# Four of sixteen state indices of a selective scan get their input from a GpSimd multiply in the channels' own layout

## The reference, cut to what matters

```python
delta = jax.nn.softplus(dt + b_dt[None, :, None])
A = -jnp.exp(A_log)

def step(state, inp):
    d_t, b_t, c_t, u_t = inp
    dA = jnp.exp(d_t[..., None] * A)
    state = dA * state + (d_t * u_t)[..., None] * b_t[:, None, :]
    y_t = jnp.einsum('bdn,bn->bd', state, c_t)
    return (state, y_t)
```

## Time and profile before

| | |
|---|---|
| median of 3 runs | 1421.58 us (1421.44 to 1421.61) |
| the profiled execution | 1421.13 us |
| its span, first to last instruction | 1419.3 us |
| scan stage, first to last scan | 608.5 to 1401.7 us |
| one middle chunk | 100.7 us |
| PE, DVE, ACT, POOL busy in the whole span | 95%, 71%, 62%, 60% |

### The profile page before, as it was taken

One profiled execution on the slowest core, in us unless ns is written; L12 is line 12 of the kernel. 1 busy time (PEld: TensorE's weight loads), 2 busy tenths in 40 slices (PEclk: granted clock), 3 DMA queues, 4 the chain that ended last, 5 costly groups with the idle time before them and its releaser, 6 DMA issues.

```text
span 1419.3 us, 24153 instructions
## 1 busy us (share of the span) xinstructions
PE 1353.3 (95%) x8924; PEld 1080.8 (76%) x8924; DVE 1010.3 (71%) x1358; ACT 879.9 (62%) x1459; POOL 844.6 (60%) x474
## 2 busy tenths in 40 slices
PE   7999999999999999999899999999999999999998
PEld 4445559999999988957677777777778678678787
DVE  7755543232233343488998998998989989989897
ACT  3211121111111132589998999999999999999983
POOL 3222211222222212368978988888889889889994
PEclk9999999999999999999999999999999999999999
DMA  9921126676667664331531642623534524613522
GB/s 298 397 100 59 52 78 227 252 268 249 248 257 267 254 229 171 146 88 46 104 77 46 133 93 51 145 61 77 119 75 90 105 62 91 134 47 88 136 74 62
DMA packets 111012, 197.07 MB, mean 139 GB/s; under 512 B 57519, under 2 KB 84271, under 8 KB 106038
## 3 DMA queue, kind: packets, MB, share of 16 engines
q1 hardware_dynamic: 93814, 146.75, 31.2%
q0 software_dynamic: 17088, 48.85, 16.0%
HBM read 141.78 MB, written 31.00 MB: 122 GB/s over the span
## 4 chain that ended last, share of the span: by engine, by line
PE 70%; ACT 12%; DVE 12%; issue 5%; DMA 0%; DVEq 0%; SPq 0%; ACTq 0%
PE bank L1666 17%; PE bank L1840 9%; PE bank L1611 9%; PE bank L1679 9%; DVE hst L1509 6%; ACT dA L947 5%; PE bank L1860 5%; ACT dbuT L936 4%; PE bank L1720 4%; PE bank L1767 2%; PE bank L1848 2%; PE bank L1731 2%; PE bank L1750 2%; PE bank L1712 2%; PE bank L1641 2%
## 5 line engine op out<-in xcount | busy, mean ns | idle before, releaser
L1509 DVE TENSOR_TENSOR_SCAN hst<-dA,carry,bank 128x512 f32<-128x512 f32 x512 | 631.8, 1267 | 56.3 <-PE bank L1840 38.0
L740 POOL TENSOR_TENSOR hst<-hst,c_bc 128x2048 f32<-128x2048 f32 x127 | 543.0, 4308 | 57.9 <-DVE hst L1509 48.9
L947 ACT ACTIVATE dA<-delta,negA 128x512 f32<-128x512 f32 x512 | 353.5, 712 | 8.0 <-DVE hst L1509 7.5
L1840 PEld LDWEIGHTS bank<-ident,dbuT 128*128 128x128 f32 x2048 | 240.0, 141 | 139.3 <-issue 66.0
L1840 PE MATMUL bank<-ident,dbuT 128*128 128x128 f32 x2048 | 311.3, 276 | 32.7 <-DVE hst L1509 28.5
L936 ACT ACTIVATE dbuT<-duT,bT 128x512 f32<-128x512 f32 x382 | 268.9, 710 | 5.4 <-PE bank L1840 5.4
L1666 PEld LDWEIGHTS bank<-f_sb,w_gu 128*128 128x128 f32 x2240 | 256.0, 192 | 4.7 <-issue 2.1
L1666 PE MATMUL bank<-f_sb,w_gu 128*128 128x128 f32 x2240 | 256.9, 275 | 0.7 <-ACT f_sb L804 0.7
L1860 PE MATMUL bank<-ident,hst 128*128 128x128 f32 x1648 | 226.2, 273 | 0.0
L1860 PEld LDWEIGHTS bank<-ident,hst 128*128 128x128 f32 x1648 | 188.9, 141 | 0.0
L670 POOL TENSOR_TENSOR x_sb<-x_sb,neg_half 128x1 f32<-128x1 f32 x35 | 22.6, 647 | 271.4 <-DVE x_sb L1290 271.4
(11 more groups left out here) (220 smaller groups left out, 1656.0 us busy)
## 6 DMA issues: line engine op xcount, KB each, us to landing
w_gu<-in_w_gu SPq DMA_DIRECT2D x35, 2048.0 KB
c_bc<-c_rows SPq DMA_DIRECT2D x64, 512.0 KB, 4.1
hst<-hst POOLq DMA_DIRECT2D x23, 1026.0 KB, 8.6
sorted_x<-sg_a SPq DMA_DIRECT2D x12, 387.0 KB, 12.1
x_sb<-sorted_x SPq DMA_DIRECT2D x35, 129.0 KB
x_sb<-in_x SPq DMA_DIRECT2D x8, 512.0 KB, 7.7
w_d<-in_w_d SPq DMA_DIRECT2D x1, 4096.0 KB, 20.7
x_mix<-x_sb SPq DMA_DIRECT2D x1, 4096.0 KB, 30.5
```

Of the source, the lines that this page charges most:

```text
L740: pool.tensor_tensor(h[:, :, :CH], h[:, :, 1:], c, ALU.mult).then_inc(hc_ready, 1)
L947: act.activation(dA[:, at % DA_BUFS, :], delta[q % B][:, d, :], ACT.Exp, scale=negA[:, d, n:n + 1]).then_inc(dA_ready, 1)
L1509: v.tensor_tensor_scan(h[:, d, 1:], dA[:, at % DA_BUFS, :], bank[4 + u % 2][:], carry1[q % B][:, n, d:d + 1], ALU.mult, ALU.add).then_inc( ...
L1840: ins = pe.transpose(bank[4 + u % 2][:, i * P:(i + 1) * P], dbuT[(DS * q + n) % DBU_BUFS][:, i, d * P:(d + 1) * P], ident[:])
```

## The change

For the indices in `DIRECT` (0, 2, 6, 9; in the first chunk 3, 6, 9) du*B_n is made in the channels' own layout. SP copies B's row to all partitions (`b_bc`, one buffer; B's rows are now stored beside C's in `bc_all`), and POOL multiplies the whole du, kept in a tile of its own, by it in one instruction of 128x2048 (`make_dbu`), three states ahead. The scans of these indices read that buffer from SBUF and no bank. ACT spreads all twelve others, POOL none. The merges at 9 and 13 go; PE adds those states singly. `duT` and `bias_b` are kept once instead of twice, which makes room. The tables of units are new, and ACT's spreads and PE's turns have tables of their own (`ACT_SPREAD`, `PE_TURN`).

```diff
-POOL_SPREADS = (5, 6, 8, 11)
-SPREAD_LEAD = 4
+DIRECT = (0, 2, 6, 9)
+DIRECT_LEAD = 3
-MERGES = {1: 0, 9: 8, 13: 12}
-LAST_MERGES = {1: 0, 9: 8}
+MERGES = {1: 0}
+LAST_MERGES = {1: 0}
+FIRST_DIRECT = (3, 6, 9)
+LAST_DIRECT = (0, 2, 6, 9)
...
+        du = sb(l1, "du", [P, DB, CH])
+        b_bc = sb(l1, "b_bc", [P, CH])
...
+            def load_b(g):
+
+                if g in DIRECT_NO:
+                    q, n = divmod(g, DS)
+                    sp.wait_ge(c_stored, 16 * TPC * (q + 1))
+                    wait_past(sp, direct_made, DIRECT_NO[g])
+                    sp.dma_start(b_bc[:], bc_all[q:q + 1, n, :].broadcast_to([P, CH])).then_inc(b_loaded, 16)
...
                     wait_freed(pool, t, f"DL{d}")
-                pool.tensor_tensor(du[:, d, :], delta[(t + 1) % B][:, d, :], xc[:, d, :], ALU.mult).then_inc(du_ready, 1)
+                if t > 0:
+                    wait_full(pool, t - 1, f"DUT{d}")
+                if t >= 0:
+                    pool.wait_ge(direct_made, sum(g < DS * (t + 1) for g in DIRECT_NO))
+                to = du_first if t < 0 else du
+                pool.tensor_tensor(to[:, d, :], delta[(t + 1) % B][:, d, :], xc[:, d, :], ALU.mult).then_inc(du_ready, 1)
...
-            def spread_du(q, n):
...
+            def make_dbu(g):
+
+                wait_slot(pool, g)
+                if g >= DS:
+                    pool.wait_ge(du_ready, DB * (g // DS) + DB - 1)
+                pool.wait_ge(b_loaded, 16 * (DIRECT_NO[g] + 1))
+                rows = b_bc[:].unsqueeze(1).broadcast_to([P, DB, CH])
+                pool.tensor_tensor(dbuT[g % DBU_BUFS][:], du[:], rows, ALU.mult).then_inc(direct_made, 1)
...
+            pool.wait_ge(delta_first, DB)
+            pool.wait_ge(xc_ready, DB)
+            pool.wait_ge(down_ready, SLOTS)
+            pool.tensor_tensor(du[:], delta[0][:], xc[:], ALU.mult).then_inc(du_again, 1)
+            pool.wait_ge(du_again, 1)
...
                     if n in merges(q):
                         merge(q, n)
+                    if g + DIRECT_LEAD in DIRECT_NO:
+                        make_dbu(g + DIRECT_LEAD)
...
-                    v.wait_ge(dbu_full, at + 1)
+                    g = DS * q + n
+                    if g in DIRECT_NO:
+                        v.wait_ge(direct_made, DIRECT_NO[g] + 1)
+                        dbu = dbuT[g % DBU_BUFS][:, d, :]
+                    else:
+                        v.wait_ge(dbu_full, FULL[at])
+                        dbu = bank[4 + u % 2][:]
...
-                    v.tensor_tensor_scan(h[:, d, 1:], dA[:, at % DA_BUFS, :], bank[4 + u % 2][:],
+                    v.tensor_tensor_scan(h[:, d, 1:], dA[:, at % DA_BUFS, :], dbu,
                                          carry1[q % B][:, n, d:d + 1], ALU.mult, ALU.add).then_inc(scan_done, 1)
```

More of the change, by code:

```diff
@@ L150 @@
 CLAIMS = sorted(JOBS, key=lambda name: CLAIMED[name])
+ACT_ORDER, PE_ORDER = [[] for _ in range(UNITS * CHUNKS)], [[] for _ in range(UNITS * CHUNKS)]
+for q in range(CHUNKS):
+    units = [u for u in range(UNITS) if u // DB not in direct(q)]
+    planned = q > 0 and direct(q) == DIRECT
+    for k, u in enumerate(units):
+        at = u - AHEAD if not ACT_SILU + 1 < u - AHEAD <= ACT_SILU + PIECES else ACT_SILU + 1
+        if q or u >= 2 * TPC:
+            ACT_ORDER[UNITS * q + (ACT_SPREAD[k] if planned else at)].append((q, u))
+        if q or u > 2:
+            PE_ORDER[UNITS * q + (PE_TURN[k] if planned else u - 1)].append((q, u))
 FIRST_CLAIMS = {"X0": 5, "X1": 6, "X2": 5, "X3": 6, "XN0": 5, "XN1": 6, "DT": 5, "DL0": 5, "DL1": 6, "DL2": 5, "DL3": 6,
@@ L172, in tiles_of @@
     return slice(lo, lo + TPC)
-def pool_spreads(q):
-    return POOL_SPREADS if q + 1 < CHUNKS else LAST_SPREADS
+DIRECT_NO, SPREAD_NO, FULL = {}, {}, {}
+LAST_USER, bank_user = {}, [None, None]
+for g in range(DS * CHUNKS):
+    if g % DS in direct(g // DS):
+        DIRECT_NO[g] = len(DIRECT_NO)
+        continue
+    SPREAD_NO[g] = len(SPREAD_NO)
+    for d in range(DB):
+        at = DB * g + d
+        FULL[at] = DB * SPREAD_NO[g] + d + 1
+        LAST_USER[at], bank_user[at % 2] = bank_user[at % 2], at
 PLACE = {}
@@ L1021, in _ @@
                         decay(q, u + 1)
-                    if u == ACT_SILU + 1:
-                        for piece in range(u + AHEAD, u + AHEAD + PIECES):
-                            spread_du(q, piece)
-                    elif u + AHEAD < UNITS:
-                        if (q > 0 or u + AHEAD >= 2 * TPC) and not ACT_SILU + 1 < u <= ACT_SILU + PIECES:
-                            spread_du(q, u + AHEAD)
-                    elif q + 1 < CHUNKS:
-                        spread_du(q + 1, u + AHEAD - UNITS)
+                    for of, piece in ACT_ORDER[unit(q, u)]:
+                        spread_du(of, piece)
                     slot(q, u)
@@ L1829, in spread @@
                 n, d = divmod(u, DB)
-                on_pool = pool_spreads(q)
-                if d == 0 and n in on_pool:
-                    pe.wait_ge(dbuT_pool, TPC * (len(POOL_SPREADS) * q + on_pool.index(n) + 1))
-                elif d == 0:
-                    made = sum(k not in on_pool for k in range(n + 1))
-                    pe.wait_ge(dbuT_act, TPC * (DS - len(POOL_SPREADS)) * q + TPC * made - FIRST_PIECES)
-                    if q == 0 and n == 0:
+                g, at = DS * q + n, unit(q, u)
+                if g in DIRECT_NO:
+                    return
+                if d == 0:
+                    pe.wait_ge(dbuT_act, TPC * (SPREAD_NO[g] + 1) - FIRST_PIECES)
+                    if g == 0:
                         pe.wait_ge(dbuT_first, FIRST_PIECES)
-                wait_past(pe, scan_done, unit(q, u - 1))
+                if LAST_USER[at] is not None:
+                    pe.wait_ge(scan_done, LAST_USER[at] + 1)
                 for i in range(TPC):
```

156 lines of the change are left out of this document (78 added, 78 removed), and 11 rows, old and new, of the table SUM_AT.

## The result

The changed kernel takes 1613.05 us (median of 4 runs, 1612.7 to 1615.09), the kernel before 1421.51 us in the same runs: the ratio is 1.135, 95% interval 1.133 to 1.137. The forecast of 1585.8 us had the direction and the mechanism right and the size 27 us too low. The profiled execution took 1615.09 us, with a span of 1613.3, against 1421.13 and 1419.3 before: 194.0 us more.

What follows compares the result with a forecast made beforehand. PE, DVE and ACT were taken to set the period in turn. A middle chunk became 93.3 + 2 + 27.3 = 122.6 us; all chunks added 164.7 to 1421.1, giving 1585.8 us, range 1485 to 1645.

Steps and rivals of the forecast that it cites:

- one instruction a state: Rival: at each direct state DVE waits for one POOL instruction, +11.4 us a middle chunk, 1509 us; chance 0.13.
- every scan: Rival: exclusion at every direct scan, with POOL always holding another multiply, 1650 us; chance 0.09 near 1640.
- the three places: Earlier trace at 39.35, 36.66 and 584.86: DVE or POOL instructions held or lengthened beside the other, 584.86's from 0.40 to 3.56 us.
- The walk: POOL's list beside DVE's through a middle chunk's four direct states: 27.3 us of standing DVE.
- (a): State 6: DVE waits out 2.3 us of C(4), scans once, then waits 4.2 for C(5): 6.5 us lost.
- (b): State 9: DVE waits for 1.5 us of C(7), all of C(8) and a du piece of 1.3 us: 7.0.
- (c): State 0, POOL furthest behind: DVE waits for part of C(14), C(15) and index 2's multiply: 9.9 us.
- (d): State 2: DVE waits only for C(1), which starts some 0.3 us ahead of its arrival: 3.9 us.
- the credit for idle time: Middle chunk: PE and ACT catch up while DVE stands, so 2 of DVE's 7.4 us idle time remain.
- the sum: All chunks' growth added: five middle chunks +109.5, chunk 6 +22.5, first +12.8, last +19.9; +164.7 us in all.

Runs made afterwards that it cites:

- The second probe: The kernel before with six short DVE and POOL stages added behind its last store, some with a DMA issue ahead of POOL's multiplies; one scan stood 11.41 us.
- the 98.1 us chunk: The changed kernel with direct scans reading what is left in bank 4 or 5 instead of the SBUF buffer: 1410.08 us, ratio 0.992.
- the run that raised it: The changed kernel with PE also transposing du*B for the direct states, which nothing reads: 1627.64 us, ratio 1.145.
- the third kernel with the decay in a bank: The changed kernel with direct states' decays written to banks 4 and 5, two units later in ACT's list: 1487.48 us, ratio 1.047.

## Why the prediction was right, and where its sizes were off

**The mechanism.** It forecast that DVE and POOL exclude each other at the direct scans, with ends that coincide with POOL's, a direct mean of 2.5 us or more, bank scans at 1.27, C multiplies up to 1.2 us longer, and chunks of 112 to 128 us. Measured: 2.71, 1.27, 5.07 against 4.19, and 126. Two runs close the argument from both sides: the operand alone makes the kernel before slow (1542), and the changed kernel without it is fast (1410). The rivals with one instruction a state (1509) and with every scan (1650) fall with the 12.55 us scan and with the three free scans behind it. One of the three places that the forecast rested on was not of its kind: the instruction of 584.86 is a `tensor_scalar` with a single tensor in SBUF, and not a pair of two. The second probe shows that one held as well, so the reading did no harm.

**The holds.** The walk gave 27.3 us a middle chunk; DVE's busy time shows 23.0. By its letters, taken from each direct scan's length over 1.25: (a) state 6, 3.9 and not 6.5; (b) state 9, 4.6 and not 7.0; (c) state 0, 11.3 and not 9.9; (d) state 2, 3.5 and not 3.9. At 6 and 9 the walk had DVE arrive while an earlier C multiply had 2.3 and 1.5 us left. In the trace that one was over at 6, and at 9 the hold began with C(8). As I read it (no run took it apart), a hold keeps DVE back while POOL works off its backlog, and the walk carried the backlog of the old pace along. At 0, where most stands on POOL, it was the other way round. The first chunk lost 13.9 (walk: 17.4), the last 25.6 (25.5). Over the eight chunks DVE's busy time rose from 732.2 to 910.2 us, 178.0 us of standing, against 206.7 in the sum.

**The step that failed is the credit for idle time.** "PE and ACT catch up while DVE stands, so of the 7.4 us that DVE idles now I leave 2". DVE's idle time is 9.8 us in the middle chunk (126.1 less 116.3), 9.6, 9.3 and 9.3 in the first, seventh and last, nowhere less. Over the eight chunks it is 78.2 us, where it was 61.0 before and the sum left 19: 42 us of credit were given, and 17 were lost on top. Of these 59 us the smaller holds gave back 29, and what lies outside the chunks 1; the rest is the 29 us that the profiled execution lies above 1585.8. So the sum came as near as it did because two errors partly cancelled, which is luck. PE does not catch up in a hold. It stands too, 17.5 us a chunk in waits for scans, and starts when DVE starts; that it can't work ahead because its two banks are full and its additions wait for scans is read from the lists, and no run took it apart. A single hold a chunk already leaves DVE idle for 8.6 us and not 7.4. Without holds, in the 98.1 us chunk, the same lists have DVE idle for 5.6 us. Part of the wait may be the lower clock, whose transposes take 292 ns and not 275; the run that raised it also gave PE more to do, so that stays open.

**PE, ACT and POOL.** PE's busy time was to fall to 92.5 and 75% of a chunk; it rose to 100.0, 79%, at the clock of 0.89. At 1.00, in the kernel of 98.1 us, it is 92.9. ACT is at 95.2 (75%), as costed at nothing. POOL has 93.9 and not 91, mostly since its direct multiplies take 4.69 us and not 4.2. That is no wait for scans. In the third kernel with the decay in a bank, where no scan has both operands in SBUF, they take as long:

```profile
L763 POOL TENSOR_TENSOR dbuT<-du,b_bc 128x2048 f32<-128x2048 f32 x4 | 18.7, 4679 | 0.0
```

So the C multiply's 4.2 us was the wrong price for them. B's rows, the new waits and the single merge cost nothing that shows, as said.

## What to carry to other kernels

Before moving work to GpSimd, look at what VectorE reads meanwhile: in these runs a scan with one operand in PSUM did not notice GpSimd, and one with two in SBUF stood for the GpSimd instructions that read SBUF. The price is not a rate but GpSimd's backlog at that moment, so walk both lists in order and count what GpSimd still has queued, and give no credit for engines catching up unless their buffers let them run ahead. A buffer moved to PSUM to avoid this costs depth: two banks in place of eight buffers cost 77 us here at the best of three places and 152 at the worst, counted from the 1410 us kernel, of the port's 203.

## What was not expected of the hardware

- GpSimd lets a waiting VectorE instruction in between two of its own (its next multiply then takes 5.07 us instead of 4.16), but not always, and a DMA issue of its own ahead is neither needed for the exception nor enough. In the second probe one scan stood 11.41 us behind an issue, and in the changed kernel the first scan of all seven later chunks took 11.9 to 13.8 us, six of them behind an issue and the one of 11.94 without. With a quarter of the direct multiply, behind the same issue, a scan that arrived in GpSimd's second instruction was let in ahead of the third. The 3.56 us of the earlier trace rows may be another case: a DMA issue ends right ahead of POOL's three multiplies there. What decides is open.
- A `tensor_scalar` on VectorE with one SBUF tensor is held like a scan with two, in the second probe: 10.36 us behind an issue, where it takes 0.47 with GpSimd idle. Beside GpSimd's memset, which holds no scan, it took 0.97.
- GpSimd's short pieces take turns with VectorE: four pieces of 128x512 and three scans take 4.48 and 4.43 us side by side, so the loss is not a whole chain of pieces.
